# Gated graph layer of a four-layer graph and expert network on Trainium2: row operations on ScalarE, biases in fused weights, router two turns behind

## The reference, cut to what matters

```python
h    = layernorm(x)                          # no gain, no bias
deg  = adj.sum(-1) + 1e-6;  n = deg ** -0.5
f    = n * (h @ theta)
hom  = n * (adj @ f)                         # smoothed part
het  = h @ W_h
gate = sigmoid(h @ W_t + b_t)
x    = x + elu(gate * hom + (1 - gate) * het)
```

## Time and profile before

| | kernel before |
|---|---|
| median of 3 runs | 3785.49 us |
| the profiled execution's own time | 3794.2 us |
| its span, first to last instruction | 3792.4 us |
| busy in the span: PE, DVE, ACT, POOL | 75%, 62%, 42%, 25% |
| mean granted TensorE clock | 0.88 of full speed |
| the graph layer's turns: start of the first and of the last difference (L1385) | 964.13 us, 1195.98 us |

### The profile page before, as it was taken

The page is one execution under the profiler, slowest core; times in us unless marked ns, Lnnn a source line. Parts: engine busy times, 40 slices in busy tenths (PEclk is TensorE's granted clock), DMA queues, the critical chain, the costliest instruction groups (busy, mean ns, idle before and its releaser), DMA issues. The chain is left out here.

```text
span 3792.4 us, 72109 instructions
## 1 busy us (share of the span) xinstructions
PE 2844.5 (75%) x19592; PEld 2209.9 (58%) x19593; DVE 2344.2 (62%) x6847; ACT 1578.6 (42%) x4694; POOL 938.1 (25%) x922
## 2 busy tenths in 40 slices
PE   4999956880674780679999999688895777739991
PEld 3666646780664780646666666455563454429991
DVE  5555544555786457467777777388884677734554
ACT  1333323442222342644444444266663555514442
POOL 0222232551233240501111111100001133333441
PEclk9999978995876895889999999799997798859996
DMA  4111102224110212300000000000001000001224
GB/s 150 38 35 34 34 27 63 72 70 141 61 50 31 55 54 67 128 1 1 0 0 0 0 0 1 19 18 22 22 17 52 7 22 19 23 30 56 62 62 144
DMA packets 164812, 160.09 MB, mean 42 GB/s; under 512 B 19664, under 2 KB 150736, under 8 KB 164048
## 3 DMA queue, kind: packets, MB, share of 16 engines
q1 hardware_dynamic: 143184, 113.87, 10.1%
q0 software_dynamic: 21504, 44.74, 3.4%
HBM read 107.48 MB, written 51.05 MB: 42 GB/s over the span
## 5 line engine op out<-in xcount | busy, mean ns | idle before, releaser
L1045 POOL DMA_INDIRECT y_rows<-ffn_e_rows_out,ffn_e_scatter_at x352 | 337.9, 960 | 512.5 <-DVE ffn_e_rows_out L1073 309.1
L1175 PE MATMUL bank<-ffn_e_xT,ffn_e_mine 128*128 128x128 f32 x3360 | 443.3, 279 | 23.8 <-issue 10.7
L1175 PEld LDWEIGHTS bank<-ffn_e_xT,ffn_e_mine 128*128 128x128 f32 x3360 | 407.9, 194 | 35.4 <-issue 31.6
L803 POOL DMA_INDIRECT sorted_rows<-ffn_r_h,ffn_r_slot x320 | 312.0, 975 | 262.2 <-issue 262.2
L1185 PE MATMUL bank<-constants,ffn_e_hid 128*128 x1968 | 278.6, 275 | 0.7 <-DVE ffn_e_hid L1093 0.4
L1093 DVE TENSOR_TENSOR ffn_e_hid<-ffn_e_act,bank 128x256 f32<-128x256 f32 (+1 forms) x280 | 135.7, 485 | 193.0 <-ACT ffn_e_act L1134 162.4
L1185 PEld LDWEIGHTS bank<-constants,ffn_e_hid 128*128 128x128 f32 x1968 | 248.0, 192 | 2.0 <-issue 1.3
L2353 ACT ACTIVATE gnn_prob<-bank,gnn_low 128x256 f32<-128x256 f32 x512 | 193.6, 489 | 52.4 <-DVE gnn_low L2271 52.4
L1134 ACT ACTIVATE ffn_e_act<-bank 128x256 f32<-128x256 f32 (+1 forms) x280 | 121.5, 434 | 213.7 <-PE bank L1175 212.4
L2271 DVE TENSOR_REDUCE gnn_low<-bank 128x2 f32<-128x512 f32 x256 | 158.9, 683 | 63.5 <-PE bank L2447 63.4
L1130 ACT ACTIVATE ffn_e_mine<-constants 128x256 f32 (+1 forms) x346 | 158.2, 457 | 94.5 <-issue 79.9
(11 more groups left out here) (478 smaller groups left out, 6873.3 us busy)
## 6 DMA issues: line engine op xcount, KB each, us to landing
g_adj<-in_adjT SPq DMA_DIRECT2D x48, 512.0 KB, 4.0
ffn_e_rows_in<-sorted_rows SPq DMA_DIRECT2D x352, 66.0 KB
ffn_c_y<-y_rows SPq DMA_DIRECT2D x80, 256.0 KB, 2.9
gnn_adj<-in_adjT SPq DMA_DIRECT2D x16, 512.0 KB, 4.0
constants<-in_ffn SPq DMA_DIRECT2D x1, 6281.0 KB, 18.5
y_rows<-ffn_e_rows_out,ffn_e_scatter_at POOLq DMA_INDIRECT x352, 2.2
constants<-in_ffn SPq DMA_DIRECT2D x1, 5206.0 KB, 15.6
sorted_rows<-ffn_r_h,ffn_r_slot POOLq DMA_INDIRECT x320, 2.3
```

Of the source, the lines that this page charges most:

```text
L803: g.indirect_dma_start(self.c.sorted_rows, bass.IndirectOffsetOnAxis(self.slot[par][:, k, j:j + 1], 0), self.h[par][:, j, :], None).then_i ...
L1045: g.indirect_dma_start(c.y_rows, bass.IndirectOffsetOnAxis(scatter_at[par][:, k:k + 1], 0), rows_out[par][:, k, :], None).then_inc(scatter ...
L1175: ins = pe.matmul(chunk(part, ch), chunk(weights[:, i * HALF:(i + 1) * HALF], ch), x, start=True, stop=True)
```

## The change

Only `phase_gnn1` is changed. In words:

- Row operations move from DVE to ACT: the normalised rows (`rows_h`, four activations of 127 columns each, with scale and bias), and the scaling of the theta product by `norm` (`scaled_f`, four activations). ACT also takes Relu of the mix (`pos`), and exp of the whole mix; DVE then needs no `pos`/`neg` split: it adds min(exp, 1) and then relu - 1 to `c.X`, in place, without the copy.
- The bias add is gone. Column 127 of `h` is set to 1 once. Since a normalised row sums to zero, its last entry can be had from the other 127; so the weights are folded once, at the start of the phase: one matmul with (identity minus a matrix whose last row is ones), three copies, and b_t as last row of W_t (`fused`). The tanh reads PSUM directly and writes SBUF (`gate`).
- PE order in turn t: router logits of t-2, transposes and degrees of t+1, aggregate of t, weight products of t+1 (gate first, then het, then f), rank of t-2, router transposes of t-1.
- ACT order in turn t: hT of t+1, router exp of t-2, tanh and het copy of t+1, exp and Relu of t, router rows of t-1, f of t+1, h of t+2, router hT of t-1.
- DVE order in turn t: choice of t-2, degree of t+1, difference, scale and mix of t, router shift of t-1, gates and places of t-2, the two sums into x, statistics and their reduction for t.
- POOL order in turn t: norm of t+1, dispatch of t-2, root of t. SP is unchanged.
- `every_turn` is called with `begin=3`, so four turns are written out ahead of the loop. The rank has a PSUM bank of its own.

The core of the diff:

```diff
             @block.vector
                 def turn(t, par, first, last):
...
+                    rows_, now = ds(t * TT, TT), counted(v, t + 1)
+                    if routed(t):
+                        behind = counted(v, t - 1)
+                        choose(t - 2, par, behind)
+                    if not last:
+                        degrees(t + 1)
+                    v.wait_ge(agg_ps, now)
+                    v.wait_ge(het_ready, now)
                     for k in range(TT):
                         ins = v.scalar_tensor_tensor(diff[:, k, :], B[5][:, k * P:(k + 1) * P], norm[par][:, k:k + 1],
                                                      het[par][:, k, :], ALU.mult, ALU.subtract)
...
+                    then(v, v.scalar_tensor_tensor(diff[:], gate[par][:], 1.0, diff[:], ALU.add, ALU.mult), scaled, now)
+                    v.scalar_tensor_tensor(mixed[par][:], diff[:], 0.5, het[par][:], ALU.mult, ALU.add).then_inc(mixed_ready, 1)
+                    if not first:
+                        route.vector_shift(v, t - 1, 1 - par, counted(v, t))
+                    if routed(t):
+                        route.vector_gates(v, t - 2, behind)
+                        route.vector_places(v, t - 2, par, behind)
+                    v.wait_ge(exp_ready, now)
+                    v.scalar_tensor_tensor(c.X[:, rows_, :], ex[:], 1.0, c.X[:, rows_, :], ALU.min, ALU.add).then_inc(x_sum, 1)
+                    v.wait_ge(x_sum, 2 * t + 1)
+                    v.scalar_tensor_tensor(c.X[:, rows_, :], pos[:], -1.0, c.X[:, rows_, :], ALU.add, ALU.add).then_inc(x_sum, 1)
...
             @block.scalar
+                def rows_h(t):
+                    wait_past(a, hT_ps, t)
+                    for k in range(TT):
+                        at = ds(t * TT + k, 1)
+                        ins = a.activation(h[:, k:k + 1, 0:D - 1], c.X[:, at, 0:D - 1], ACT.Identity, bias=c.shift[:, at], scale=c.rstd[:, at])
+                    ins.then_inc(h_ready, 1)
...
+                def scaled_f(t, par):
+                    a.wait_ge(norm_ready, t + 1)
+                    a.wait_ge(f_ps, t + 1)
+                    for k in range(TT):
+                        ins = a.activation(f[par][:, k, :], B[1][:, k * P:(k + 1) * P], ACT.Copy, scale=norm[par][:, k:k + 1])
+                    ins.then_inc(f_ready, 1)
...
                 def turn(t, par, first, last):
                     if not last:
                         evac_hT(t + 1, 1 - par)
+                    if routed(t):
+                        route.scalar_exp(a, t - 2)
+                    if not last:
+                        gates(t + 1, 1 - par)
+                    a.wait_ge(mixed_ready, t + 1)
+                    wait_past(a, x_sum, 2 * t)
+                    a.activation(ex[:], mixed[par][:], ACT.Exp)
+                    a.activation(pos[:], mixed[par][:], ACT.Relu).then_inc(exp_ready, 1)
                     if not first:
                         route.scalar_rows(a, t - 1, 1 - par)
                     if not last:
+                        scaled_f(t + 1, 1 - par)
+                    if not (isinstance(t, int) and t >= TURNS - 2):
+                        rows_h(t + 2)
                     if not first:
                         route.scalar_hT(a, t - 1)
...
             @block.tensor
                 def turn(t, par, first, last):
+                    if routed(t):
+                        route.tensor_logits(pe, t - 2)
+                    if not last:
+                        to_features(t + 1)
+                        degrees(t + 1, 1 - par)
                     pe.wait_ge(f_ready, t + 1)
+                    wait_past(pe, below, t)
...
                     ins.then_inc(agg_ps, 1)
                     if not last:
                         front(t + 1, 1 - par)
+                    if routed(t):
+                        route.tensor_rank(pe, t - 2)
                     if not first:
                         route.tensor_hT(pe, t - 1, 1 - par)
```

More of the change, by code:

```diff
@@ L1299, in phase_gnn1 @@
         adj = [sb(f"adj{i}", [P, 4, NODES]) for i in range(2)]
-        one = sb("one", [P, 1])
+        one, ones, differ, fused = sb("one", [P, 1]), sb("ones", [P, P]), sb("differ", [P, P]), sb("fused", [P, 3, D])
         deg = sb("deg", [P, TT])
@@ L1303, in phase_gnn1 @@
         f = [sb(f"f{i}", [P, TT, D]) for i in range(2)]
-        gpre = [sb(f"gpre{i}", [P, TT, D]) for i in range(2)]
         het = [sb(f"het{i}", [P, TT, D]) for i in range(2)]
-        diff, neg, pos, ex = sb("diff", [P, TT, D]), sb("neg", [P, TURN]), sb("pos", [P, TURN]), sb("ex", [P, TURN])
-        one_ready = sem("one_ready")
+        gate = [sb(f"gate{i}", [P, TT, D]) for i in range(2)]
+        mixed = [sb(f"mixed{i}", [P, TT, D]) for i in range(2)]
+        diff, ex, pos = sb("diff", [P, TT, D]), sb("ex", [P, TT, D]), sb("pos", [P, TT, D])
+        one_ready, differ_ready, fused_ps, fused_ready = sem("one_ready"), sem("differ_ready"), sem("fused_ps"), sem("fused_ready")
         adj_ready = [sem(f"adj_ready{i}") for i in range(2)]
@@ L1335, in turn @@
                 def turn(t, par, first, last):
-                    if not first:
-                        route.pool_rstd(g, t - 1)
                     if not last:
                         degree_norm(t + 1, 1 - par)
-                    if not first and not (isinstance(t, int) and t == 1):
+                    if routed(t):
                         route.pool_dispatch(g, t - 2, par)
-                every_turn(g, turn)
-                route.pool_rstd(g, TURNS - 1)
+                    route.pool_rstd(g, t)
+                every_turn(g, turn, begin=3)
                 route.pool_dispatch(g, TURNS - 2, 0)
@@ L1349, in _, with degrees @@
             def _(v):
-                v.memset(one[:], 1.0).then_inc(one_ready, 1)
-                def front(t, par):
+                v.memset(h[:, :, D - 1:D], 1.0)
+                v.memset(ones[:], 1.0)
+                then(v, v.memset(one[:], 1.0), one_ready, 1)
+                then(v, v.tensor_scalar(ones[:], ones[:], last_row, None, ALU.mult), one_ready, 2)
+                v.tensor_tensor(differ[:], c.ident[:], ones[:], ALU.subtract).then_inc(differ_ready, 1)
+                v.wait_ge(fused_ps, 1)
+                weights = B[5][:, 0:3 * D].rearrange("p (k d) -> p k d", k=3)
+                v.tensor_copy(fused[:, 0, :], weights[:, 0, :])
+                v.tensor_copy(fused[:, 2, :], weights[:, 2, :])
+                v.scalar_tensor_tensor(fused[:, 1, :], w["b_t"], last_row, weights[:, 1, :], ALU.mult, ALU.add).then_inc(fused_ready, 1)
+                def degrees(t):
                     v.wait_ge(deg_ps, t + 1)
@@ L1355, in front, with choose @@
                     v.tensor_scalar(deg[:], B[7][:, 0:TT], 1e-6, None, ALU.add).then_inc(deg_ready, 1)
[L1356 to L1370, removed]
+                degrees(0)
                 route.vector_begin(v)
+                def choose(t, par, now):
+                    route.vector_first(v, t, par, now)
+                    route.vector_chosen(v, t, now)
                 def turn(t, par, first, last):
[L1374 to L1383, removed]
+                    rows_, now = ds(t * TT, TT), counted(v, t + 1)
[6 more added lines that the diff above has]
+                    v.wait_ge(het_ready, now)
                     for k in range(TT):
@@ L1386, in turn @@
                                                      het[par][:, k, :], ALU.mult, ALU.subtract)
[L1387 to L1401, removed]
@@ L1402, in turn @@
-                    if not (isinstance(t, int) and t >= TURNS - 2):
-                        normalised(t + 2)
-                    if not first:
[L1405 to L1409, removed]
+                    then(v, ins, below, now)
+                    v.wait_ge(gate_ready, now)
@@ L1458, in to_features, with degrees @@
                     ins.then_inc(hT_ps, 1)
[L1460 to L1461 removed]
+                def degrees(t, par):
                     pe.wait_ge(adj_ready[par], 8 * (t - par) + 16)
```

67 lines of the change are left out of this document (38 added, 29 removed).

## The result

| | before | changed |
|---|---|---|
| median of 7 runs | 3785.49 us | 3818.43 us |
| ratio, changed to before | | 1.0075 [1.0053, 1.0096] |
| span of the profiled execution | 3792.4 us | 3813.1 us |
| mean granted TensorE clock | 0.880 | 0.876 |
| the graph layer's phase, from its start to that of the next | 295.56 us | 331.01 us |

A forecast was written before the change was run, and what follows sets the result against it. DVE's list was taken to bound the kernel before, a closed chain through ACT and PE after. 3 + 14 + 14 x 18.4 - 231.85 = 42.8 us, added to 3785.5, gave 3828 us; range 3788 to 3850.

The forecast's parts named there:

- DVE's list: DVE's work in one graph-layer turn, said to bound the kernel before; predicted to fall from 15.73 to 10.1 us.
- The closed chain: Mix, ACT's rows through hT, PE's logits through aggregate, DVE's difference, all in series; 13.7 us a turn upper clock, 18.2 lower.
- lower level: PE's granted clock at 0.50, 1.2 GHz; predicted from logits through aggregate, pricing that leg at 9.59 us instead of 5.10.
- hand-overs: Passing between engines along the turn's serial steps, priced at 0.1 us a turn.
- The clock: Step predicting PE slow from logits through aggregate, recovering around the start of the weight products; 18.4 us a turn, 60%.
- The clock stays up throughout: Rival: PE at the upper clock in every turn, its gaps being shorter than before; 13.7 us a turn, 3760 us, 10%.
- The aggregate and half the degrees at the upper level too: Rival: these PE steps at the upper clock as well; about 15.6 us a turn, 3789 us, no change, 12%.
- The first difference: Head of the graph layer: DVE's first difference comes 3 us later (2.3 to 3.7).
- The first turn: Graph layer's first turn, without router rows, hT or logits but with one table load; 12 to 15.6 us, taken as 14.
- The steady turns: Graph-layer turns after the first, summed as 14 of 18.4 us each.
- The tail: After the last difference: same router steps for the last two turns, no difference claimed (-1 to +2 us).
- The other edits: Router choice, POOL's root, adjacency load, weight fold, claimed hidden; more turns written out, 0 to 2 us, taken as 0.

The follow-up runs named there:

- e4: Changed kernel plus 34 unread matmuls a turn in PE's two gaps around the router's transposes; ratio to before 0.9931, phase 275.4 us.
- e2: Changed kernel with the four rows of h back on DVE behind the router's shift; 3786.3 us, ratio to before 0.9996.
- e3: Changed kernel with PE's degrees of t+1 moved from ahead of the aggregate to between het and f weight products; 3757.97 us, ratio to before 0.9914.
- e6: e5 plus 12 unread matmuls behind the router's transposes, on the slower chip; 4010.83 us against 4059.23 before.
- e5: Changed kernel with hT ahead of h, degrees between weight products, turn 0's transposes ahead of its degrees; slower chip, 4014.41 us against 4059.23 before.
- e9: Same kernel as e5, run on the first kind of chip; 3740.78 us, ratio to before 0.9858.

## Why the prediction was right, and where not

**The bound and its replacement.** Right. DVE's list left the path: its work is 51% of an 18.2 us turn, 9.3 us, against the 10.1 predicted. One reading was too strong: before, DVE worked 101.5 us in 124, some 12.9 in a turn of 15.73, so it stood nearly 3 us a turn and not only the 0.70 for exp (0.52 of it for POOL's `norm`, at 1079.95). Most of what can be named (exp, `norm`) is a step that DVE itself sets off, so the 15.73 holds as the length of DVE's list with its waits. The closed chain took its place, step by step in the turn shown:

| leg | predicted, us | measured, us |
|---|---|---|
| difference, scale, mix, to exp (with het late) | 2.63 + 0.1 + 0.2 | 3.19 (1074.17 to 1077.36) |
| ACT, exp to the end of hT | 5.88 | 5.70 (1077.36 to 1083.06) |
| PE, logits to the end of the aggregate, lower level | 9.59 | 9.64 (1083.12 to 1092.76) |
| hand-overs | in the first leg | 0.10 |
| turn | 18.4 | 18.63 here, 18.19 on average |

The average is (1219.84 - 983.36) / 13, the 13 turns between the second difference and the fifteenth. ACT's leg is shorter by the rows of `f`: 1.12 us, where I had 1.28 from L1275. In the first leg `het` held exp up by 0.5 here rather than 0.2, behind weight products of 3.80 us. In the turn of 17.78 us between the fourteenth and the fifteenth difference these took 3.04, exp started 0.5 earlier, and the last part of the aggregate was at the upper level too (3.39 instead of 3.76).

**The clock.** Right, and e4 is what shows it. The logits, transposes, degrees and aggregate ran at the lower level in the steady turns read, the first transposes of the kind at 975.38 (1.11 us). "The clock stays up throughout" was given 13.7 us a turn; e4, which forces it, measured 13.7. The Trainium skill (TensorE: Matmul & The Clock Gate, HAM oscillation) made that rival. Its rule, as I had read it, doesn't fit this case: the gaps of 2.04 and 2.37 us are both shorter than the 3.10 of the earlier trace rows, and the granted clock went from 1.00 to 0.50 all the same.

**ACT's rows against DVE's.** The Trainium skill (ScalarE: Activation LUTs, rules for kernel authors) keeps such work on VectorE. Here that holds for `h`, by e2, though for a reason that no load shows: ACT was busy 43%, 7.8 us a turn, but 5.7 of these lay in series between the mix and the logits. The set of `f` costs the same on either engine: 1.12 us on ACT, and 1.12 on DVE before (L1362, at 1079.95).

**One rival was mis-sized.** "The aggregate and half the degrees at the upper level too" was given 15.6 us a turn, 3789, no change. By the prediction's own legs it is 17.2 less 1.73 for the aggregate and about 0.8 for half the degrees: 14.7 a turn, about -9 us, 3776. That lies below the range's lower end, so the 12% given to no change rest on a wrong sum. The forecast does not use it.

**What was mis-sized.** The sum was +42.8, the phase gave +35.4:

- *The first difference*, +3 (at most 3.7): 967.94 - 964.13 = 3.81, of which 0.43 is the phase's later start.
- *The first turn*, 14: 983.36 - 967.94 = 15.42, the upper end of my 12 to 15.6. Its PE part ran wholly at the lower level, after PE had waited 4.80 us for `h`. I had taken the middle.
- *The last turn*: not in the sum as a turn of its own, and this is the step that failed. In it no transposes and degrees of a next turn (0.88 + 3.28) stand ahead of the aggregate, and no `h` of t+2 (1.55) ahead of hT. It took 1232.22 - 1219.84 = 12.38 instead of 18.4: -6.0.
- *The steady turns*, 13 x (18.19 - 18.4) = -2.7.
- *The tail*, 0: from the last difference to the next phase 36.61 us after, 36.97 before: -0.4.

Together 3.81 + 15.42 + 236.48 + 12.38 - 231.85 - 0.36 = 35.9, less the later start 35.4. The missed last turn is most of the error, and it was to be had from the diff: `if not last` stands on the calls of PE, and `t >= TURNS - 2` on `rows_h`.

**The other edits.** Hidden, as said. The adjacency was never waited for, and POOL's root, 1084.78 in the turn shown, had no one waiting. The fused weight product lay beside the wait for the first adjacency (944.42, 1.65 us). Only one table load stands in the layer (L1456 at 970.34, 1.28 us). That more turns are written out can't be seen in any row.

## What to carry to other kernels

When work moves off the bound engine, walk one turn from a buffer back to itself on the new order: ACT at 43% and DVE at 51% busy were the picture of a chain. What lies on it counts in full: taking `h` off it was worth 1.83 us a turn, taking the degrees off it 4.6, part of that through the clock. Price every leg on TensorE at both of its clock levels: here the waits of the chain came with 9.59 us of TensorE work instead of 5.10. And write the first and the last turn into the sum on their own: `if not last` takes work off the path.

## What the runs showed of the hardware

- **One gap's length doesn't decide the clock.** In e3 the logits took 1.87 us (lower level) behind a gap of 2.37 and 1.05 (upper level) behind one of 2.45, fourteen microseconds later. In both cases a gap (0.38 and 0.68) and one set of transposes (0.66) stood before. What tells the two turns apart isn't shown.
- **A busy PE can stay at the lower level.** In the changed kernel PE ran without a pause from 1083.20 to 1092.50 at a granted 0.50, through 16 degrees of one column (3.41 us) and the aggregate. In e6 there are no degrees in that place, and PE was busy for 9.40 of 9.50 us at 0.50 (1139.00 to 1148.50), fill and aggregate included.
- **Useless matmuls paid.** 34 unread ones a turn took the phase from 331.0 to 275.4 us. Where the chain was already short, 12 of them were worth little: 251.5 to 244.3. On the slower chip they brought nothing (251.4 and 253.5), and there three turns stayed at the lower level in spite of them.
- **Chips differ by 7% on the same kernel** (3790.18 and 4059.23 us), and not evenly: e5 and e9, the same kernel, have the same phase on both, 251.4 and 251.5 us.
